# Attention of the next 512 tokens run in bursts between the feed-forward products, in quarter-array tiles, with the gate and up banks rescaled in place between groups

## What is computed

```python
def xattn(xq, c, Wq, bq, Wk, bk, Wv, bv, Wo, bo):   # 8 heads of 64
    q, k, v = proj(Wq, bq, xq), proj(Wk, bk, c), proj(Wv, bv, c)   # 'oi,bil->bol', a 64x64 matrix each
    p = softmax(einsum('hbdk,hbek->hbde', qh, kh) / sqrt(64))
    return proj(Wo, bo, merge(einsum('hbde,hbek->hbdk', p, vh)))
def ffn(y):                                  # W = (int - zero) * scale, in groups of 128 rows
    return (silu(y @ Wgate) * (y @ Wup)) @ Wdown         # 512x1792, 512x1792, 1792x512
x = x + xattn(layernorm(x), ctx, ctx, ...)
x = x + ffn(layernorm(x), ...)
```

## Time and profile before

| | us |
|---|---|
| median of 3 runs (464.47 to 465.43) | 464.55 |
| span of the profiled execution | 461.8 |
| PE busy | 422.4 (91%) |
| DVE busy | 416.2 (90%) |
| POOL busy | 369.3 (80%) |
| ACT busy | 301.2 (65%) |

### The profile page before, as it was taken

The page is one execution under the profiler, slowest core; times in us unless marked ns, Lnnn a source line. Parts: engine busy times, 40 slices in busy tenths (PEclk is TensorE's granted clock), DMA queues, the critical chain, the costliest instruction groups (busy, mean ns, idle before and its releaser), DMA issues.

```text
span 461.8 us, 9217 instructions
## 1 busy us (share of the span) xinstructions
PE 422.4 (91%) x3314; PEld 345.0 (75%) x3314; DVE 416.2 (90%) x688; ACT 301.2 (65%) x495; POOL 369.3 (80%) x254
## 2 busy tenths in 40 slices
PE   2888778888989999999999999999999999999994
PEld 2667666767866888888888888888888888888863
DVE  3699999999999899999899999979999898999996
ACT  1455567645548777767877766787776678766741
POOL 3046756554536999999998999999899999999994
PEclk9999999999999999999999999999999999999998
DMA  5598987666500000000001000000100000010003
GB/s 176 198 362 272 375 293 255 194 195 211 159 2 0 3 0 1 0 1 1 23 26 46 1 0 1 1 23 24 45 2 1 0 2 23 25 45 1 0 1 91
DMA packets 18038, 35.57 MB, mean 77 GB/s; under 512 B 2406, under 2 KB 4622, under 8 KB 17994
## 3 DMA queue, kind: packets, MB, share of 16 engines
q1 hardware_dynamic: 17198, 34.78, 22.4%
q10 hardware_dynamic: 668, 0.22, 0.2%
q0 software_dynamic: 128, 0.00, 0.0%
HBM read 30.71 MB, written 4.28 MB: 76 GB/s over the span
## 4 chain that ended last, share of the span: by engine, by line
PE 70%; DVE 23%; ACT 2%; issue 2%; DMA 1%; POOL 1%; ACTq 0%; POOLq 0%; DVEq 0%
PE banks L658 33%; PE banks L659 32%; DVE st L701 4%; DVE p_sb L754 3%; DVE pe_ L740 2%; DVE sm L744 2%; ACT pe_ L467 2%; DVE mx L738 2%; DVE kT L722 2%; DVE qT L722 2%; DVE nm L716 2%; PE banks L639 1%; PE banks L633 1%; DMA xn<-in_L_xattn_Wo 1%; DVE ri L748 1%
## 5 line engine op out<-in xcount | busy, mean ns | idle before, releaser
L848 DVE SCALAR_TENSOR_TENSOR acc<-banks,sgu,acc 128x512 f32<-128x512 f32 x232 | 162.2, 744 | 25.6 <-PE banks L659 20.1
L658 PE MATMUL banks<-xT,wgu 128*128 128x512 f32 x448 | 177.8, 397 | 0.6 <-DVE acc L848 0.4
L659 PE MATMUL banks<-xT,wgu 128*128 128x512 f32 x448 | 175.8, 392 | 0.0
L528 ACT ACTIVATE acc<-banks,sgu 128x512 f32<-128x512 f32 x216 | 130.8, 687 | 4.2 <-PE banks L659 4.2
L372 POOL TENSOR_TENSOR acc<-acc 128x1024 f32<-128x1024 f32 x52 | 125.5, 2414 | 9.9 <-DVE acc L848 9.8
L848 DVE SCALAR_TENSOR_TENSOR yT<-banks,sd,yT 128x512 f32<-128x512 f32 x179 | 126.2, 742 | 0.8 <-PE banks L659 0.8
L658 PEld LDWEIGHTS banks<-xT,wgu 128*128 128x128 f32 x448 | 84.1, 188 | 20.3 <-DVE acc L848 2.1
L659 PEld LDWEIGHTS banks<-xT,wgu 128*128 128x128 f32 x448 | 84.2, 188 | 18.1
L658 PE MATMUL banks<-hr,wd 128*128 128x512 f32 x224 | 88.8, 397 | 2.8 <-DVE yT L848 1.6
L659 PE MATMUL banks<-hr,wd 128*128 128x512 f32 x224 | 88.1, 393 | 0.0
L494 ACT CAST hr<-h_sb 128x512 fp32r<-128x512 f32 x56 | 34.8, 622 | 74.1 <-POOL h_sb L378 74.1
(11 more groups left out here) (67 smaller groups left out, 446.0 us busy)
## 6 DMA issues: line engine op xcount, KB each, us to landing
wz_in<-z_gu SPq DMA_DIRECT2D x16, 448.0 KB, 5.6
ctx_sb<-in_ctx SPq DMA_DIRECT2D x16, 256.0 KB, 4.5
out<-x_sb SPq DMA_DIRECT2D x16, 256.0 KB, 2.0
wq_in<-in_L_ffn_gate_w SPq DMA_DIRECT2D x8, 448.0 KB, 4.1
wq_in<-in_L_ffn_up_w SPq DMA_DIRECT2D x8, 448.0 KB, 4.0
wq_in<-in_L_ffn_down_w SPq DMA_DIRECT2D x14, 256.0 KB, 2.8
wz_in<-z_d SPq DMA_DIRECT2D x14, 256.0 KB, 4.0
x_sb<-in_x SPq DMA_DIRECT2D x3, 1024.0 KB, 8.6
```

Of the source, the lines that this page charges most:

```text
L528: act.activation(dst, bank, ACT.Copy, scale=scale_of(u)).then_inc(s_ea, 1)
L658: pe.matmul(bank, w, parts[0], start=True, stop=False)
L659: mm = pe.matmul(bank, w, parts[1], start=False, stop=True)
L848: dve.scalar_tensor_tensor(dst, bank, scale_of(u), dst, ALU.mult, ALU.add).then_inc(s_ev, 1)
```

## The change

The two phases are folded into each other. Only the attention of the first four tiles (`PRE`), and the first part of tile 4, stands ahead of the feed-forward steps. The rest is cut into bursts: `QK` projects q and k of a tile, `SV` does values and scores, `M` is the product of Wo and the softmax, `A` the product with the values, `MA` is `A` of one tile and `M` of the next. `burst_after` sets each behind a place q of the feed-forward list.

There are 236 places. At a place stand one gate and one up group of a step (`step_at`: steps with an even number at even places, the others at odd ones, so that a step's four groups stand two places apart) and, from place 12 on, one down unit (`down_at`). PSUM is divided up: banks 0 to 3 hold gate and up of two steps, banks 4 and 5 are the `ring` of the down, X and Y units, and banks 6 and 7 are for the bursts.

Gate and up of a step stay in their bank for all four groups: between groups ACT multiplies the bank by the ratio of the two groups' scales (`rescale`), in place, and PE adds the next group on top. At the end ACT takes tanh and DVE forms the gate from it (`gated`), in place of the silu; ACT scales up (`take_u`); POOL multiplies (`product`) and now makes the high part too (`high`). The projections work on quarters of the array, 64x64, four positions in turn. The division of the softmax goes from DVE to POOL (`weigh`), and so does the first layer norm's application from tile 5 on. Pieces of weights hold 1,024 elements to a partition; from piece 8 on, 13 in all, they are dequantised beside the steps, every second one by DVE alone.

The diff has 1,670 lines; this is its core, without blank lines:

```diff
-    ORDER = [("G", 0), ("U", 0), ("G", 1), ("U", 1), ("silu", 0), ("G", 2), ("U", 2), ("D", 0), ("D", 1),
-             ("G", 3), ("U", 3), ("D", 2), ("D", 3), ("high", 0)]
...
+    def step_at(q):
+        n, r = (2 * (q // 8), q % 8) if q % 2 == 0 else (2 * ((q - 3) // 8) + 1, (q - 3) % 8)
+        return (n, r // 2) if 0 <= n < NS else None
+    def down_at(q):
+        return divmod(q - LATE, NC) if 0 <= q - LATE < NC * NS else None
+    LATE = 12
+    PLACES = 4 * NS + LATE
+    PER = 4 * NI
...
+    for c in range(NCH - 1):
+        a, b, cc, d = (CT * (c + 1) + i for i in range(CT))
+        plan = [("QK", b), ("M", a), ("SV", b), ("QK", cc), ("MA", b), ("SV", cc), ("QK", d), ("MA", cc),
+                ("SV", d), ("QK", d + 1), ("MA", d), ("A", d), ("SV", d + 1)]
+        for j, (kind, t) in enumerate(plan):
+            if t < NT:
+                q = PER * c + 8 * (j // 2) + (1 if j % 2 == 0 else 5)
+                burst_after[q] = (kind, t)
+                if kind == "MA":
+                    x_after[q + 6] = t - 1
+                if kind == "A":
+                    x_after[q + 6] = t
+    for c in range(1, NCH):
+        for i in range(CT):
+            y_after[PER * c + LATE + 1 + 2 * i] = CT * (c - 1) + i
...
+    ln1_after = {q - 7: t for q, t in qk_after.items() if q >= 7}
...
+    ring = [("X", t) for t in range(PRE)]
+    for q in range(PLACES):
+        if down_at(q):
+            n, b = down_at(q)
+            ring.append(("D", n, b))
+            if n == NS - 1 and b >= 1:
+                ring.append(("YB", b - 1))
+        if q in x_after:
+            ring.append(("X", x_after[q]))
+        if q in y_after:
+            ring.append(("Y", y_after[q]))
+    ring.append(("YB", NC - 1))
+    slot = {u: i for i, u in enumerate(ring)}
...
+            def high(n):
+                pool.wait_ge(s_h, n + 1)
+                if n >= 2:
+                    pool.wait_ge(s_full, slot["D", n - 2, NC - 1] + 1)
+                else:
+                    pool.wait_ge(s_bV, PRE)
+                pool.tensor_copy(hr[:, n % 2, 0, :], t_sb[:, n % 2, :]).then_inc(s_hi, 1)
+            def low(n):
+                pool.wait_ge(s_hi, n + 1)
+                pool.tensor_tensor(hr[:, n % 2, 1, :], t_sb[:, n % 2, :], hr[:, n % 2, 0, :].bitcast(F32),
+                                   ALU.subtract).then_inc(s_lo, 1)
...
+            for q in range(PLACES):
+                at = step_at(q)
+                if at and at[1] == NG - 1:
+                    product(at[0])
+                    high(at[0])
+                    low(at[0])
+                if q - 3 in sv_after:
+                    weigh(sv_after[q - 3])
+                if q in res_after:
+                    rstd(1, res_after[q])
+                if q in ln1_after:
+                    rstd(0, ln1_after[q])
+                if q - 1 in ln1_after:
+                    norm1(ln1_after[q - 1])
+                for k in piece_after.get(q, ()):
+                    if not by_vector(k):
+                        less_zeros(k)
...
+            def rescale(n, g):
+                it = n % NI
+                for bank, full, done, m in ((G_BANK[n % 2], s_G, s_Gs, 0), (U_BANK[n % 2], s_U, s_Us, 1)):
+                    act.wait_ge(full[n % 2], NG * (n // 2) + g + 1)
+                    act.activation(banks[:, bank, :], banks[:, bank, :], ACT.Copy,
+                                   scale=ratio[:, m, g, it:it + 1]).then_inc(done[n % 2], 1)
...
+                for m, src in enumerate((xn[:, t % 2, :], ctx_of(t))):
+                    for c in range(NC):
+                        for b, hp in TURNS:
+                            r, k = HALVES[b], HALVES[hp]
+                            h = 2 * c + hp
+                            mm = pe.matmul(banks[k, at + b, (m * NC + c) * D:(m * NC + c + 1) * D],
+                                           src[r, h * Lh:(h + 1) * Lh], wT[r, m, :], start=True, stop=True)
...
+            def free_slot(u):
+                if slot[u] >= 2:
+                    pe.wait_ge(s_free, slot[u] - 1)
+                return banks[:, unit_bank(u), :]
...
+                        pe.wait_ge(s_sub, PRE + 1)
+                for bank, full, done, last, m in ((G_BANK[n % 2], s_G, s_Gs, s_gt, 0),
+                                                  (U_BANK[n % 2], s_U, s_Us, s_uf, 1)):
+                    if g:
+                        pe.wait_ge(done[n % 2], (NG - 1) * (n // 2) + g)
+                    elif n >= 2:
+                        pe.wait_ge(last, n - 1)
+                    w = wgu[:, m, g, it * P:(it + 1) * P]
+                    pe.matmul(banks[:, bank, :], w, xT[:, c % 2, 0, g, :], start=g == 0, stop=False,
+                              skip_group_check=True)
+                    pe.matmul(banks[:, bank, :], w, xT[:, c % 2, 1, g, :], start=False, stop=True,
+                              skip_group_check=True).then_inc(full[n % 2], 1)
...
+            def shift(m, t):
+                dve.wait_ge(s_rs[m], t + 1)
+                dve.tensor_scalar(nm[:, m, t:t + 1], mv[:, m, t, 0:1], rs[:, m, t:t + 1], -1.0,
+                                  ALU.mult, ALU.mult).then_inc(s_nm[m], 1)
...
+            def take_down(n, b):
+                dve.scalar_tensor_tensor(y, bank, sd[:, it, b:b + 1], y, ALU.mult, ALU.add).then_inc(s_free, 1)
...
-                        dst = acc[:, n % 2, a, g % chains, :]
-                        wait_read(dve, (kind, n, g - chains))
-                    dve.scalar_tensor_tensor(dst, bank, scale_of(u), dst, ALU.mult, ALU.add).then_inc(s_ev, 1)
...
+            for q in range(PLACES):
+                at = step_at(q)
+                if at and at[1] == NG - 1:
+                    gated(at[0])
+                if down_at(q):
+                    n, b = down_at(q)
+                    take_down(n, b)
+                    if n == NS - 1 and b >= 1:
+                        add_last(b - 1)
+                if q in x_after:
+                    rest_x(x_after[q])
+                if q in y_after:
+                    add_y(y_after[q])
+                if q in qk_after:
+                    take_qk(qk_after[q])
+                if q - 1 in sv_after:
+                    less_max(sv_after[q - 1])
+                if q - 3 in sv_after:
+                    invert(sv_after[q - 3])
+                if q - 1 in res_after:
+                    shift(1, res_after[q - 1])
+                if q in res_after:
+                    residual(res_after[q])
+                    stats(1, res_after[q])
+                if q - 1 in ln1_after:
+                    shift(0, ln1_after[q - 1])
+                if q in ln1_after:
+                    stats(0, ln1_after[q])```

What moves can be seen in three places of the engines' lists (a row is a line of the kernel, the instruction, what it writes and reads, its size, what it waits for, and how often it stands there in a row).

**PE, where the second phase begins, before.** `p_sb`, `qT`, `kT`, `aT` and `v_sb` belong to the attention of a tile, `xT` with `wgu` are gate and up products. The last rows of the attention of tile 14 and the first units of the feed-forward phase:

```order
L593 MATMUL banks<-wT,p_sb 64x64 [waits s_ate,s_p]
L593 MATMUL banks<-wT,p_sb 64x64 x15
L581 MATMUL banks<-kT,qT 64x64 [waits s_sub,s_ke,s_qe]
L581 MATMUL banks<-kT,qT 64x64 x15
L604 MATMUL banks<-v_sb,aT 64x64 [waits s_x1,s_ve,s_ate]
L604 MATMUL banks<-v_sb,aT 64x64 x15
L658 MATMUL banks<-xT,wgu 128x512 [waits s_qe,s_x0lo,s_deq]
L659 MATMUL banks<-xT,wgu 128x512
L658 MATMUL banks<-xT,wgu 128x512 [waits s_ke]
L659 MATMUL banks<-xT,wgu 128x512
```

More of the change, by code:

```diff
@@ L315, in _ @@
[L315 to L327 removed]
+            load_ctx(3)
```

1228 lines of the change are left out of this document (635 added, 593 removed).

## The result

The changed kernel takes 488.25 us (median of 4 runs, 486.91 to 490.21) against 464.51: a ratio of 1.052, 95% interval 1.048 to 1.056, so 5.2% slower. The forecast was 460.8 with a range up to 473. The profiled execution has a span of 486.4 us, where the sum of the terms had given 458.0: 28.4 us are missing.

The account below looks back on a forecast made before the run. Before, DVE paced the attention and PE alone the feed-forward phase; the terms 55.0 + 305.0 + 10.6 + 50.1 + 7.0 + 15.0 + 15.3 summed to 458.0 us, 2.75 above the span gave 460.8 us, 8-in-10 range 442 to 473.

Parts of the forecast that it names:

- the start: Part ahead: first bias addition at 12.5 us, POOL giving a tile every 8 us; feed-forward phase starts at 55.0 us.
- the end: After the last full place: last product, four down and four Y units, last DMA; 15.3 us.
- full matmuls: Feed-forward phase on PE: 1,324 gate, up and down matmuls of 0.2304 us each; 305.0 us.
- Rival C: Part ahead longer, from late zeros, weights or bias loads or PE's lower clock: start 65 us, time 471, chance 0.13.
- The repeated wait: Places 17 and 41 of three chunks: POOL's late power stops DVE's shift, PE waits 3.5 or 1.5 us; 15.0 us.
- The first waits: Early feed-forward places: PE waits 5 us for tile 5's norm, and ACT's pace in places 2 to 11 costs 2; 7.0 us.
- The pure steps: Ordinary feed-forward places: costed at nothing, cover 0.1 to 0.5 us a place; small waits up to 10 us left to the range.
- Bursts and transposes: PE in the feed-forward phase: 10.6 us for X and Y units, 50.1 for 68 sets of 0.59 in 37 bursts.
- A (waits absorbed): Feed-forward phase: bursts let other engines catch up and the shift stop stays under PE's slack; 443 us, chance 0.25.
- B (ACT the bound): Feed-forward phase: ACT's in-place PSUM operations decide from 0.77 us each; at 0.80 us 473 us, chance 0.12.
- The sign: Whole kernel: 3.8 us or 0.8% faster than before; chance of faster 0.55, slower 0.38.

Follow-up runs that it names:

- the two-load kernel: Changed kernel with q and k biases fetched in two loads instead of eight and spread by one DVE copy; 475.4 us (1.023).
- PE kept busy: The three edits plus matmuls nobody reads where PE waits for POOL's division in the part ahead; 453.15 us, in the side-by-side repeat 454.31 against 454.63.
- the three edits: Changed kernel with two bias loads, POOL's power ahead of the high part, and tile 5's norm ahead of the zeros; 453.7 us (0.975), again 454.6 (0.977).
- the one with the reordered power: Changed kernel with POOL making the second norm's power ahead of the high and low parts; 470.4 us (1.011).

## Why the prediction was wrong

Two steps failed: the start, and the small waits that were put at nothing. With +16.5 for the start, +12.0 for PE's waits, 0.5 more at the end and 0.6 less in full matmuls they make up the 28.4 us.

**The start (55.0 us).** This step failed most, by 16.5 us. "I take 12.5 us for its successor, since it waits for q and k as now but two small loads earlier" looked at when the loads are asked for, not at what they are: eight loads of 128 rows instead of two. Measured, the first division ends at 34.7 us where I had 22.4: 12.3 us, all of which the two-load kernel gave back. The later divisions came at distances of 8.2, 10.6 and 8.2 us where I had 8.0, 7.8 and 7.5, and the rest of the way took 9.7 against 9.3. Of these 4.2 us, 2.8 are a stop of PE that the trace calls issue, in the middle of a projection. The rest fits PE's sets of 1.1 us at 1.2 GHz, where I had costed PE in this part at nothing: with PE kept busy a tile takes 7.25 us instead of 8.23. That is also under the 8 us that I had given POOL; its division takes 1.04 us, and I had 1.3. Rival C named late bias loads and the lower clock, both of which were true, but priced them at 10 us together and gave them 13 in 100.

**The repeated wait (15.0).** Right in mechanism, places and size: 14.5 us measured for the six, 3.36 and 1.48 for single ones against 3.5 and 1.5; POOL's high part took 0.64 us on average and 0.61 at its shortest (assumed 0.8; the 769 ns that the prediction quoted as the best case is above it). What the term left out is the lower clock that came with the three long ones: taking the waits away was worth 17.0 us.

**The first waits (7.0).** 3.5 us at the first burst against 5 (by the prediction's own times, 55.9 to 61.4, it should have said 5.5). The norm was ready 5.5 us behind the first gate matmul and not 6.4, as the division had ended earlier and the norm took 0.76 and not 1.0; and PE came 2.1 us behind it and not 0.9, since its four matmuls ran at 1.2 GHz. ACT's pace in places 2 to 11, put at 2 us, shows as two waits for `t_sb`, 0.4 and 0.5 us.

**The pure steps (nothing).** This is the second step that failed. "They are in the range, not in the sum", up to 10 us: 16 us came, 10.0 of them in twelve waits for down banks and `t_sb`, and those of the first chunk stayed in every kernel with the other edits (8.6 us in the first chunk of the three edits). A cover of 0.1 to 0.5 us a place was no cover in a chunk in which DVE and POOL also subtract zeros.

**Bursts and transposes (60.7).** Equal in the changed kernel, by luck: a burst at 2.4 GHz is cheaper than forecast, and the bursts at 1.2 GHz made up for it. Rows of the changed kernel, a burst with two sets at 2.4 GHz:

```profile
88.15 0.40 PE L712 MATMUL banks<-xT,wgu 128*128 128x512 f32 x1
88.48 0.66 PE L637 MATMUL banks<-ctx_sb,wT 64*64 64x256 f32 x8
88.96 0.64 PE L629 MATMUL banks<-qkT 64*64 64x64 f32 x32
89.53 0.50 PE L710 MATMUL banks<-xT,wgu 128*128 128x512 f32 x1
89.87 0.40 PE L712 MATMUL banks<-xT,wgu 128*128 128x512 f32 x1
```

From 88.15 to 89.87, less two full matmuls, are 1.26 us; the prediction's 2 x 0.59 + 0.27 gives 1.45. The 0.59 from the earlier trace rows may already have held a part of the way out; no run parts the two.

**The rivals.** A (waits absorbed) fell: the stop in `shift` shows in full. B (ACT the bound) fell: 0.662 us an operation, below the 0.77 that decides, and ACT is busy 70%. C held in kind. None let C, small waits and the clock come together, and the range ended 15 us short, though each was in the text. **The sign** hung on 3.8 us, and either miss alone was more. Undoing one was not enough: the two-load kernel is still at 475.4 us and the one with the reordered power at 470.4; with all three edits the same design is faster than before.

## What to carry over

When a change multiplies a load, count its rows and not only its issues, and ask what stands first in line behind it: here eight loads of 32 KB held back a whole kernel by 12 us. An in-order engine that computes a tiny value for another should do so ahead of any operation of its own that can wait; moving one 0.55 us instruction in POOL's list was worth 17 us. And where three engines each have a few tenths of a microsecond to spare per place, put the small waits into the sum.
